# Normed attention: queries and keys projected transposed, mean squares by a product with a head selector, all squares on ScalarE

## The reference, cut to what matters

```
q = x @ Wq; k = ctx @ Wk; v = ctx @ Wv          (128 -> 16 heads x 64)
q = q * rsqrt(mean(q*q over the 64 of a head) + 1e-5) * q_norm_w
k = k * rsqrt(mean(k*k over the 64 of a head) + 1e-5) * k_norm_w
x = x + (softmax(q k^T / 8 + mask) v) @ Wo
```

## Time and profile before

| | |
|---|---|
| median of three runs | 1232.67 us |
| profiled execution, its own time | 1232.76 us |
| span of its trace | 1231.0 us |
| TensorE busy | 1027.4 us (83%) |
| VectorE busy | 855.5 us (69%) |
| ScalarE busy | 576.6 us (47%) |
| GpSimd busy | 222.0 us (18%) |
| mean granted clock of TensorE | 0.924 |

### The profile page before, as it was taken

One profiled execution on the slowest core, in us unless ns is written; L12 is line 12 of the kernel. 1 busy time (PEld: TensorE's weight loads), 2 busy tenths in 40 slices (PEclk: granted clock), 3 DMA queues, 4 the chain that ended last, 5 costly groups with the idle time before them and its releaser, 6 DMA issues.

```text
span 1231.0 us, 32393 instructions
## 1 busy us (share of the span) xinstructions
PE 1027.4 (83%) x11974; PEld 816.6 (66%) x11974; DVE 855.5 (69%) x1903; ACT 576.6 (47%) x1119; POOL 222.0 (18%) x243
## 2 busy tenths in 40 slices
PE   5678999969888886899899999899998673798756
PEld 5357888746556566778678877678776562467546
DVE  5565677788999996555677676687675577667455
ACT  1223344556666663343555665465655220344343
POOL 3554122100111101331100000000000122343100
PEclk9877999989999998899999999999999885699778
DMA  9200000000000000000000000000000000000001
GB/s 369 95 2 1 0 0 0 0 2 2 0 0 0 0 0 2 2 1 1 2 2 0 0 0 2 2 1 0 0 0 2 1 0 0 1 1 0 1 0 34
DMA packets 5919, 16.13 MB, mean 13 GB/s; under 512 B 729, under 2 KB 4962, under 8 KB 5218
## 3 DMA queue, kind: packets, MB, share of 16 engines
q1 hardware_dynamic: 5858, 15.29, 3.2%
HBM read 14.24 MB, written 1.05 MB: 12 GB/s over the span
## 4 chain that ended last, share of the span: by engine, by line
PE 40%; issue 23%; DVE 18%; DVEq 11%; POOL 3%; ACT 2%; POOLq 2%; PEldq 1%; PEld 1%; ACTq 0%
PE banks L1674 7%; PE banks L1747 4%; PE banks L1719 3%; PE banks L1136 3%; PE banks L900 3%; PE banks L1707 3%; DVEq L1346 2%; PE banks L1358 2%; PE banks L1117 1%; PE banks L1735 1%; DVE small L1591 1%; DVE xn L333 1%; POOL small L832 1%; DVEq L1012 1%; DVE xr L1011 1%
## 5 line engine op out<-in xcount | busy, mean ns | idle before, releaser
L352 POOL TENSOR_TENSOR rstd<-var,nhalf 128x2 f32<-128x2 f32 x72 | 57.3, 796 | 483.0 <-DVE var L326 483.0
L1682 ACT ACTIVATE work<-banks 128x512 f32<-128x512 f32 x128 | 74.9, 600 | 70.2 <-PE banks L1674 70.2
L1339 ACT ACTIVATE work<-work 128x1024 f32<-128x1024 f32 x64 | 67.7, 1058 | 55.6 <-DVEq L1335 32.0
L374 ACT ACTIVATE xT_all<-banks 128x256 f32 (+1 forms) x72 | 28.3, 393 | 133.5 <-PE banks L363 133.0
L1674 PE MATMUL banks<-xT_all,weights 128*128 (+1 forms) x384 | 86.2, 380 | 2.3 <-ACT work L1792 1.8
L1358 PE MATMUL banks<-ident,work 128*128 128x128 f32 x512 | 71.0, 290 | 16.2 <-DVE work L1349 11.2
L1674 PEld LDWEIGHTS banks<-xT_all,weights 128*128 128x128 f32 x384 | 71.5, 190 | 13.7 <-ACT work L1792 2.6
L929 ACT ACTIVATE work<-banks,weights 128x256 f32<-128x256 f32 x128 | 53.6, 470 | 57.5 <-PE banks L890 56.5
L1358 PEld LDWEIGHTS banks<-ident,work 128*128 128x128 f32 x512 | 62.9, 150 | 23.3 <-DVE work L1349 13.3
L1826 DVE TENSOR_TENSOR work<-banks,neg_mask 128x512 f32<-128x512 f32 x64 | 40.7, 685 | 52.2 <-PE banks L1707 50.6
L363 PE MATMUL banks<-ident,xn 128*128 128x128 f32 x144 | 33.6, 320 | 43.7 <-DVE xn L333 38.4
(11 more groups left out here) (311 smaller groups left out, 2413.3 us busy)
## 6 DMA issues: line engine op xcount, KB each, us to landing
weights<-wpack SPq DMA_DIRECT2D x1, 5381.5 KB, 32.1
weights<-wpack SPq DMA_DIRECT2D x1, 2060.0 KB, 13.2
weights<-wpack SPq DMA_DIRECT2D x1, 2049.0 KB, 17.5
weights<-wpack SPq DMA_DIRECT2D x1, 1160.5 KB, 19.8
x_all<-x_in SPq DMA_DIRECT2D x2, 512.0 KB, 4.8
ctxT_all<-ctxT_in SPq DMA_DIRECT2D x1, 1024.0 KB, 7.0
out<-x_all SPq DMA_DIRECT2D x8, 128.0 KB, 1.8
rows<-rows_in SPq DMA_DIRECT2D x1, 832.0 KB
```

Source lines behind the costliest of these rows:

```text
L352: g.tensor_tensor(rstd, var, nhalf[:, 0:2], ALU.pow).then_inc(rstd_ready, 1)
L1339: act.activation(sm[:, u, :], sm[:, u, :], ACT.Exp, scale=scale).then_inc(h["exp"].sem, 1)
L1682: act.activation(dst.rearrange("p c t -> p (c t)"), bank(ring.bank(f"qk{c}")), ACT.Copy) \
```

## The change

Queries and keys are now projected transposed, straight from `xT_all` and `ctxT_all` (`project`, units `qk`), so that `turn_qk`, `turned`, ScalarE's copies of turned banks and GpSimd's copy to `xs` go. Each of the eight `qk` banks holds two head pairs of 256 tokens; ScalarE copies it to `qT` or `kT` and squares it from the accumulator into a second buffer. The list `pooled` of banks that GpSimd would square is empty, so GpSimd's new function does nothing.

The sums over the 64 elements of a head, now along the partitions, are made by TensorE: 16 products of a selector (`head_sum`, 128 x 32) with the squares, four column tiles of 32 side by side, into one bank (`sums`). ScalarE takes Ln (with scale 1/64 and a bias of 1e-5) and Exp of 128 x 256 values. TensorE spreads these roots back over the partitions, times the gains q_norm_w and k_norm_w (`roots_spread`): 16 products with 32 rows, four row tiles side by side, into eight banks (`bc`). VectorE multiplies each `bc` bank into `qT` or `kT` (`scaled`, eight instructions), which takes the place of `mean_squares`, `divide` and `turned`.

The gains and the selector are made once: on VectorE behind the first pair of the expert stage (`make_gains`), and by eight products and one copy at the stage's start. The preparation of the first pair now stands in the lists as the expert stage's `follow`.

The core of the diff:

```diff
-        mixing8 = [(f"{k}{u}{n}", "a") for k in "po" for u in range(2) for n in range(2)]
         values4 = [(f"v{c}", "a") for c in range(4)]
-        att1 = pipelined(scores4, mixing8, [(f"tok{u}{c}", "a") for u in range(2) for c in range(4)],
-                         values4 + [(f"turn{u}{c}", "av"[c % 2]) for u in range(2) for c in range(4)])
+        queries8 = [(f"qk{c}", "a") for c in range(8)]
+        turned4 = [(f"p{u}{half}", "a") for u in range(2) for half in range(2)]
+        mixed4 = [(f"o{u}{b}", "a") for u in range(2) for b in range(2)]
+        scaling8 = [(f"bc{c}", "v") for c in range(8)]
+        att1 = stage([])
+        att1.pro = stage([("gains", "a")] + queries8 + [("sums", "a")] + scaling8 + values4, 1, shift=2)
+        att1.body = stage(scores4 + queries8 + [("sums", "a")] + turned4 + scaling8 + mixed4 + values4, PAIRS - 1)
+        att1.epi = stage(scores4 + turned4 + mixed4, 1)
...
                     combine(0)
+                    prog[att1][5](v)
                     with v.Fori(1, PAIRS) as p:
...
+            def heads_of(k):
+
+                j, m = k % 4, 2 * (k // 4)
+                return (qT if j < 2 else kT)[:, 4 * (j % 2) + m:4 * (j % 2) + m + 2, :]
+
...
+            def make_gains(v):
+
+                v.wait_ge(weights_in[group], 16)
+                v.memset(head_sum, 0.0)
+                for k in range(2):
+                    v.tensor_scalar(gains[:, k, :], ident[:], w("a1_norm")[:, k:k + 1], None, ALU.mult)
+                v.drain()
+                for m in range(4):
+                    ins = v.tensor_copy(head_sum[:, m, :, 2 * m:2 * m + 2], parity[:, None, :].to_broadcast([P, 2, 2]))
+                ins.then_inc(gains_made, 1)
+
+            def project(pe, ring, i, p):
+                pe.wait_ge(xt_stored, g_of(s, p) + 2 - PAIRS)
+                for c in range(8):
+                    wt, src = (wq, xT_all) if c < 4 else (wk, ctxT_all)
                     settle(pe)
-                for hp in range(8):
-                    half, c = hp % 2, hp // 2
-                    bk = bank(s.bank(f"s{u}{half}"))
-                    for b in range(2):
-                        for par in range(2):
-                            r0, o0, t0 = par * S, (par ^ half) * S, (2 * u + b) * S
-                            ins = pe.matmul(bk[o0:o0 + S, (2 * c + b) * S:(2 * c + b + 1) * S],
-                                            qT[r0:r0 + S, hp, t0:t0 + S], kT[r0:r0 + S, hp, t0:t0 + S],
-                                            start=True, stop=True)
-                    if hp >= 6:
-                        ins.then_inc(banks_filled, 1)
-
-            def project(pe, s, i):
-
-                if normed:
-                    for u in range(2):
-                        for c in range(4):
-                            src, wt = (xs, wq) if c < 2 else (cs, wk)
...
-                    return
-                for c in range(8):
-                    wt, src = (wq, xs) if c < 4 else (wk, vsrc)
-                    pe.wait_ge(*s.bank_free(i, f"qk{c}"))
+                    pe.wait_ge(*first_free(ring, i, f"qk{c}"))
                     for j in range(2):
-                        ins = pe.matmul(bank(s.bank(f"qk{c}"))[:, j * PT:(j + 1) * PT],
...
+            def sums(pe, ring, i, p):
+                settle(pe)
+                pe.wait_ge(*ring.emptied(i, "qk7"))
+                if ring is s.body and pooled:
+                    pe.wait_ge(*pool_squared.at(p - 1, 1))
+                settle(pe)
+                pe.wait_ge(*ring.bank_free(i, "sums"))
+                bk = bank(ring.bank("sums"))
+                for m in range(4):
+                    for j in range(4):
+                        ins = pe.matmul(bk[32 * j:32 * j + 32, 0:PT], head_sum[:, m, 0, :],
+                                        squares[j // 2][:, 4 * (j % 2) + m, :], start=(m == 0), stop=(m == 3),
+                                        tile_position=(0, 32 * j))
+                ins.then_inc(banks_filled, 1)
+
+            def roots_spread(pe, ring, i, p):
+                pe.wait_ge(*roots_made.at(p, 1))
+                for m in range(4):
+                    for j in range(4):
+                        name = f"bc{4 * (m // 2) + j}"
+                        if m % 2 == 0:
+                            settle(pe)
+                            pe.wait_ge(*ring.bank_free(i, name))
+                    for j in range(4):
+                        name = f"bc{4 * (m // 2) + j}"
+                        ins = pe.matmul(bank(ring.bank(name))[:, PT * (m % 2):PT * (m % 2) + PT],
+                                        gains_spread[32 * j:32 * j + 32, P * m:P * m + P],
+                                        head_roots[32 * j:32 * j + 32, :], start=True, stop=True,
+                                        tile_position=(32 * j, 0))
+                        if m % 2:
+                            ins.then_inc(banks_filled, 1)
+
...
+            def tensor_head(pe):
+                pe.wait_ge(weights_in[group], 16)
+                pe.wait_ge(gains_made, 1)
+                pe.wait_ge(*first_free(s.pro, 0, "gains"))
+                for k in range(2):
+                    for m in range(4):
+                        ins = pe.matmul(bank(s.pro.bank("gains"))[S * k:S * k + S, P * m:P * m + P],
+                                        head_sum[:, m, :, :].rearrange("p k r -> p (k r)"), gains[:, k, :],
+                                        start=True, stop=True)
+                ins.then_inc(banks_filled, 1)
+                project(pe, s.pro, 0, 0)
+                sums(pe, s.pro, 0, 0)
+                roots_spread(pe, s.pro, 0, 0)
+                values(pe, s.pro, 0, 0)
+
...
+                def part(ring, i, p, last=True):
+                    if ring is s.body:
+                        pe.wait_ge(*ring.emptied_before(i, "bc7"))
                         settle(pe)
-                        scores(pe, ring, i, 0)
-                        scores(pe, ring, i, 1)
-                    if nxt:
-                        pe.wait_ge(staged, g_of(s, p) + 2 - PAIRS)
-                        project(pe, ring, i)
-                    if this:
-                        if last and nxt:
-                            pe.wait_ge(*ring.emptied_before(i, "o11"))
-                        if last or not nxt:
-                            result(ring, None)
-                        probs_turned(pe, ring, i, p, 0, h["prob"])
-                        probs_turned(pe, ring, i, p, 1, h["prob"])
-                        mix(pe, ring, i, 0)
-                        mix(pe, ring, i, 1)
-                    if nxt:
-                        values(pe, ring, i)
-                    if nxt and normed:
-                        turn_qk(pe, ring, i, p + 1)
-                    if this:
-                        turn_normed(pe, g_of(s, p))
-                    if not nxt:
+                    scores(ring, i, 0)
+                    scores(ring, i, 1)
...
+            def projected(act, ring, i, c):
+                act.wait_ge(banks_filled, ring.filled(i, f"qk{c}"))
+                k, a = c // 4, 2 * (c % 4)
+                bk = bank(ring.bank(f"qk{c}"))
+                ins = act.activation((kT if k else qT)[:, a:a + 2, :].rearrange("p c t -> p (c t)"), bk, ACT.Copy)
+                if ring is s.pro or c not in pooled:
+                    ins = act.activation(squares[k][:, a:a + 2, :].rearrange("p c t -> p (c t)"), bk, ACT.Square)
+                ins.then_inc(act_emptied, 1)
+
+            def head_roots_made(act, ring, i):
+                act.wait_ge(banks_filled, ring.filled(i, "sums"))
+                act.activation(head_roots, bank(ring.bank("sums"))[:, 0:PT], ACT.Ln, bias=eps[:, 0:1],
+                               scale=1.0 / 64).then_inc(act_emptied, 1)
+                act.drain()
+                act.activation(head_roots, head_roots, ACT.Exp, scale=-0.5).then_inc(roots_made.sem, 1)
+
...
+            def scalar_head(act):
+                act.preload_act_table_set("natural_log_exp_and_others")
+                act.wait_ge(banks_filled, s.pro.filled(0, "gains"))
+                act.activation(gains_spread, bank(s.pro.bank("gains")), ACT.Copy).then_inc(act_emptied, 1)
+                for c in range(8):
+                    projected(act, s.pro, 0, c)
+                head_roots_made(act, s.pro, 0)
+                act.wait_ge(xn_ready, g_of(s, 0))
+                values_taken(act, s.pro, 0)
 
...
+                def part(ring, i, p, last=True):
+                    own = ring is s.body
+                    for c in range(2 * own):
+                        projected(act, ring, i, c)
+                    soft_exp(act, p, 0, scale, h)
+                    for c in range(2, 6 if own else 0):
+                        projected(act, ring, i, c)
+                    soft_exp(act, p, 1, scale, h)
+                    for c in range(6, 8 if own else 0):
+                        projected(act, ring, i, c)
+                    if own:
```

(27 more changed lines are left out.)

309 lines of the change are left out of this document (122 added, 187 removed).

## The result

| | before | after |
|---|---|---|
| median | 1232.16 us (1228.65 to 1232.94, 4 runs) | 1252.01 us (1242.89 to 1253.06, 4 runs) |
| profiled execution / its span | 1232.76 / 1231.0 us | 1252.37 / 1250.7 us |
| mean granted clock of TensorE | 0.924 | 0.919 |

The ratio of the times is 1.014, with a 95% interval of 1.0102 to 1.0178: the changed kernel is 1.4% slower. The forecast was 1227 us.

The account below looks back on a forecast made before the run. VectorE alone was taken to set the pair behind the softmax. Steady and last steps -7.3, first step +1.5, preparation -1.0, gains +0.9 sum to -5.9 us: 1227 us, 8-in-10 range 1217 to 1241.

Parts of the forecast that it names:

- The walk of the steady pair: Looped steps: timeline of engine work from scores to next scores, 28.2 us instead of 29.49, sums taking 1.9 us.
- Turned stream and the loop's end: scores again at 27.9: End of the steady pair: values done at 27.6, next pair's scores starting at 27.9 us.
- an allowance of 0.3: Steady pair: 0.3 us added for register instructions ahead of nine more waits on computed values, giving 28.2 us.
- The 0.8 us of the last step: Last step: gain of 0.8 us, from 29.04 to 28.2 us.
- a gain of 1.0: Preparation of the first pair: scores at 257.5 instead of 258.52 us, gain between 0.3 and 2.2.
- 0.9 for the gains: Making gains on VectorE behind the expert stage's first pair: 0.9 us late, at least 0, at most 1.3.
- the walk's best case: Preparation at full clock: scores at 256.3 us, the upper gain of 2.2 us.
- +1.5 predicted: First step: loss of 1.5 us, between 0 and 2.5, from a lower clock after four idle microseconds.
- one row at 0.50: Preparation: a profiled stretch with long gaps at granted clock 0.50, kept in mind when setting first scores at 257.5 us.
- A (column tiles): Sums of squares: only two column tiles run at once, +13.6 us, so 1240 us; chance 0.20.
- B (clock in the steady pair): Spread of roots: clock falls after 1.7 us idle, values and mixes some 2 us longer, 1239 us; chance 0.17.
- three signs of being wrong: Changed stage: sums over 2.8 us, loop clock under 0.97, or pair under 27 us would make the forecast wrong.

Follow-up runs that it names:

- two traces of the changed kernel: The first profile of the changed kernel and a rerun of the same kernel unaltered for a second trace; the rerun measured 1249.38 us, ratio 1.0134.
- 28 more: Changed kernel plus 28 semaphore increments without work on TensorE in the preparation's two idle stretches; 1244.15 us, ratio 1.0091.
- both edits: Changed kernel without TensorE's drain behind the values and with unread products in the idle stretches of preparation and first step; 1226.76 us, ratio 0.9953.
- either edit alone: Changed kernel with only the drain behind the values removed, 1240.05 us; or with only 29 unread products in the idle stretches, 1236.89 us.
- the other kernel: Changed kernel without the drain, with unread products, plus 32 semaphore increments at the start of TensorE's normed attention; 1237.31 us, ratio 1.0053.

## Why the prediction was wrong

The terms of the sum against the two profiles:

| | predicted | measured |
|---|---|---|
| gains and preparation, to the first scores | -0.1 us | +2.2 us |
| first step | +1.5 | +2.1 |
| five steady steps | -6.5 | +5.2 |
| last step | -0.8 | +0.1 |
| last pair | 0 | 0 |
| later stages | not in the sum | +10.1 |
| all | -5.9 | +19.6 |

Two steps failed above all: the end of the pair, and the stages beside the change that stood at nothing.

**The walk of the steady pair was right, its last step was not.** Sums of 32 records in 1.95 us (predicted 1.9), starting at 13.9 (13.5), the second half of the spread waiting for VectorE 1.36 us, VectorE 19.4 us (20), no wait for VectorE ahead of the scores. The Trainium skill (TensorE: Matmul & The Clock Gate, Part 3: Packing small matmuls) says that a weight load overlaps products in flight only when the row group differs. These products do not agree with it: four column tiles share all rows, and 32 records with their 32 loads took 1.95 us, 0.061 us each.

The failed step is "Turned stream and the loop's end: scores again at 27.9", with an allowance of 0.3. I had values done at 27.6 (measured 28.0) and then counted 0.3 us to the scores; it was 1.63. Before, the drain stood at the same place, but 32 transposes of queries and keys stood behind it. The change removed them, and left the drain next to the loop's end. I had listed what was removed as work, and never asked what the drain would cost once nothing covered it. What covered it before is not shown. In the kernel before, both halves of the transposes stood behind other waits (values, then transposes):

```profile
424.85 1.99 PE L1440 MATMUL banks<-weights,cs 128*128 128x512 f32 x4 [0.36 <-ACT work L1560]
427.74 1.96 PE L1452 MATMUL banks<-ident,weights 128*128 128x128 f32 x16 [0.90 <-ACT work L1568]
430.41 1.97 PE L1452 MATMUL banks<-ident,weights 128*128 128x128 f32 x16 [0.71 <-DVE weights L1601]
```

The scores behind them waited 1.0 to 1.3 us more for VectorE, and no run took the drain out of that kernel. Price in the changed kernel: 1.5 us in each steady pair, 9 us in all by the medians.

Without the drain the pair takes 28.1, against a forecast of 28.2, and that is partly luck: the values are done 0.4 us later than in the walk (the sums start at 13.9 behind ScalarE's last square, not at 13.5), and the scores follow 0.14 us behind them where the walk and its allowance had 0.6.

The 0.8 us of the last step was never there to be had. Ahead of the last pair's scores TensorE waits for all of ScalarE's copies (29.07 us without the drain, with 0.95 us of this wait), and the walk left this wait out.

**First step and preparation.** The idle time was foreseen, its cost mis-sized, and a wait left out. Preparation: predicted a gain of 1.0 (first scores 257.5, and 0.9 for the gains), measured a loss of 2.2 (260.67). Counted from the expert stage's last products (L914 and L908) to the first scores, which leaves out that this stage ends up to 4 us apart in different executions of the same code, the preparation took 24.0 us before, 26.6 and 28.6 in the two traces of the changed kernel, and 23.5 with its gaps filled. So even at a clock of 1.00 it gains 0.4 us, not the 2.2 of the walk's best case: the first scores stand 1.29 us behind the values, waiting for ScalarE's copies as ahead of the last pair, where the walk had 0.3. First step: +1.5 predicted, 30.06 - 27.92 = 2.1 measured. Filling the idle stretches gave 12.5 us in the median, of which the profiled executions show 4 to 6 in these two places. I had taken one row at 0.50 for one event of a known size, where the half clock in the preparation lasted 6.9 us in one execution of the changed kernel and 13.6 in the other. Making the gains cost VectorE 1.0 us of instructions. The expert stage's last products start at 234.08 with them and at 234.56 without, so nothing of the 0.9 that I had counted is seen; with up to 4 us between executions at this place, one trace of each could not show it.

**Unchanged stages.** They were not in the sum at all, and took 10 us more in the profiled execution. About half of that is stops inside the products of one line. That their places follow the count of instructions ahead of them is shown; in one trace with 28 more, these stages took 5.4 to 6.9 us less. Which position is good isn't shown: over all kernels here these stages took 744 to 758 us, in no simple order of the count.

**Rivals.** A (column tiles) was wrong, as was its price. B (clock in the steady pair) was wrong for its place: the spread's gap of 1.36 us stands at a clock of 1.00. In the profile the clock fell once behind a stop (second step) and once behind the drain's gaps (fifth step), and in the second trace of this kernel in none of the looped steps. Its sign and size (1239) were nearer than the forecast's, by another mechanism. The range left out the result because every case came from the changed stage, and no case had a cost for what stood still beside the change. Of the three signs of being wrong (slow sums, a low clock in the loop, a pair under 27 us) none was a pair that is too long.

**The sum, mended.** Changed kernel 1249 to 1252; without drain 9 less; with the idle stretches filled 12.5 less; both 1226.76, as the two apart would give (1249.4 - 9.3 - 12.5 = 1227.6). That both edits meet it is partly luck. From the expert stage's last products to the next stage the trace with both edits takes 242.1 us, against 248.8 before: a gain of 6.8, as the walk had without the 0.9 for the gains, but from other terms. The preparation gains 0.3 us (forecast 1.0), the first step gains 0.4 (it was to lose 1.5), the five steady steps gain 6.9 (6.5), the last step loses 0.1 (0.8 gain), and the last pair loses 0.8 (0). And the total needs the later stages at 745.9 us, where either edit alone left them at 754.5 and 754.9. As a forecast of the kernel that was run, 1227 was wrong by 25.

## What to carry to other kernels

When work is taken out of a loop, look at what is left next to each other: a drain with only two transposes and the loop's end behind it cost 1.5 us a pair here, and did not show in the pair of the kernel before. Look as well for places where one engine waits for another to be done with everything; a gain in the step ahead of them may be lost there. A gap in TensorE's work in front of a dense stretch is priced by the length of the half-clock stretch that can follow, not by one row of it; products that nobody reads, placed in the gap, are a cheap way to tell, but they move the code behind them too, so read their effect from the stretch and not from the total. In a long unrolled program hold 1 to 2% of the later stages' time as uncertain (744 to 758 us here) when instructions are added or removed ahead of them, and before judging a small edit move the code by a few instructions and time it again.

## Not expected of the hardware

- A drain on TensorE with only two transposes and the loop's end behind it: 1.63 us from the last product to the next pair's first, 0.14 without it.
- Stops of 0.4 to 1.9 us inside products of one line, at the same records in two executions of a program; three of them moved by exactly 28 instructions when 28 were put ahead. In the changed kernel a 16 KB instruction transfer starts 0.9 to 1.8 us ahead of each.
- Four column tiles of 32 columns with all 128 rows: 32 records of 256 columns in 1.95 us.
- Semaphore increments on TensorE are not free in a row: 32 of them left 5.25 us without a product where 0.53 had been idle before, 0.15 us each, and 3.54 us in the other kernel, 0.11 each.
